# Splitting the output layers' loads in an attention-plus-feed-forward kernel: Wo stays inside the last chunk, the rest goes behind the last block moves

## The chip, the cores and the metric

The kernel runs on one core of a Trainium2 chip. The metric is the device time of one execution in microseconds. Before the change it is 712.91 us, the median of 3 runs (712.37 to 714.04).

## The reference, cut to what matters

One recurrent attention layer: 512 query rows (M) attend to 6250 input rows (x) with 8 heads of 64, and a feed-forward layer follows. All is fp32.

```python
q = (M @ Wq.T).reshape(e, h, dh).transpose(1, 0, 2)          # M 512x512
k, v = jnp.split(x @ Wkv.T + bkv, 2, axis=-1)                # x 6250x256
sim = jnp.einsum('hid,hjd->hij', q, k) * dh ** (-0.5)
sim = jnp.where(mask, sim, -1000000000.0)                    # mask 512x6250
attn = jax.nn.softmax(sim, axis=-1)
out = jnp.einsum('hij,hjd->hid', attn, v)
out = out.transpose(1, 0, 2).reshape(e, h * dh) @ Wo.T + bo  # Wo 512x512
m = layer_norm(out + M)
ffn = jax.nn.relu(m @ W1.T + b1) @ W2.T + b2                 # W1 2048x512, W2 512x2048
z = layer_norm(ffn + m)
```

## The kernel before, in words

The 6250 inputs are cut into 7 chunks of 896 (7 tiles of 128). In each chunk the 8 heads go in 4 pairs (0 to 3), and for each pair the 512 queries go in 4 tiles. Every engine walks through the same list of steps, written by hand in `ROUNDS` and turned into a list by `chunk_schedule`; it does those steps that have work for it and passes over the others. Engines meet at semaphores only. A step is written here as letter(pair, number), so X(3,2) is the transpose of pair 3, query tile 2. The steps around the change:

- S(p,t): TensorE (PE) makes the scores, VectorE (DVE) adds the mask and takes the minimum (line 669). E: ScalarE (ACT) takes the exponential (531). X(p,t): DVE transposes 32x32 blocks of the probabilities from `prob` to `st` (679). `st` has two halves, one for query tiles 0 and 1 and one for 2 and 3. X of an even tile waits until the DMAs that read this half for the pair before have landed (semaphores `landed`).
- M(p,g) and B(p,g): the blocks in half g are moved between partition groups, from `st` to `pt`, by 16 DMAs of 112 KB: 12 issued by SP's queue (M, line 350) and 4 by ACT's queue (B, line 567). In the text "move (p,g)" is all 16.
- W(p,kt): PE multiplies `pt` with the values (853). It starts only when both moves of its pair have landed. C copies the result out of the bank, F transposes it back, A adds it to the accumulator, N divides by the softmax sum, G, T and D turn and split the normalised output, and Y multiplies it with Wo (784).
- Z(p): GpSimd (POOL) updates the maxima and sums (423 to 434), ACT makes alpha (571).
- R and Q load the next x and mask. In the last chunk they are left out. There I stands instead (SP, lines 366 to 377) at the end of pair 2's last round: after a few waits SP issues Wo (1024 KB), M (`m_res`, 1024 KB), the first two tiles of W1 and of W2 (4 times 256 KB), and the biases bo and b2 spread over 128 partitions (2 times 256 KB). O stands at the end of pair 3's last round (POOL, 463 to 470): it splits Wo into a high and a low part (465, 467) and then adds bo to M (470).

After the list of the last chunk the output layers follow: ACT (577, 581) and DVE (709, 713) split the first feed-forward tiles, DVE adds `m_res` and gathers the statistics of the layer norm (701 to 705), PE turns the result (893), and 16 hidden tiles run through PE (904 and 912), whose weights SP loads two tiles ahead.

SP's queue is one list in program order. In the last chunk SP issues M(2,0), then I, then M(2,1), M(3,0) and M(3,1). The same stretch on POOL: Z(2), O, Z(3).

Of the kernel before, what the change touches and what calls it, by code (L numbers as in the profile page):

```python
# [12 lines left out]
P = 128  # L13
# [3 lines left out]
DM = 512  # L17
# [5 lines left out]
PAIRS = HEADS // 2  # L23
U = 2 * QT
KT = 7
CHUNK = KT * P
CHUNKS = -(-N // CHUNK)
# [44 lines left out]
def chunk_schedule(first, last):  # L72

    out = []
    for p in range(PAIRS):
        for t in range(QT):
            for word in ROUNDS[p][t].split():
                kind, i = word[0], int(word[1:] or 0)
                step = (kind, p, i)
                if kind == "S":  # L80
                    step = (kind, p, t)
                elif kind == "E":
                    step = (kind, p, (t, i))
                elif kind == "X":
                    step = (kind, p, t - 1) if t else (kind, p - 1, QT - 1)
                elif kind == "V":
                    step = (kind, 0, i)
                elif kind in "NP":
                    if kind == "P" and not first or kind == "N" and last:
                        continue  # L90
                    step = ("V", 1 if kind == "N" else 0, i)
                elif kind in "WC":
                    step = (kind, p - 2, i)
                elif kind in "FA":
                    step = (kind, p - 3, i)
                elif kind in "KHL":
                    step = (kind, p + 1, i)
                elif kind in "MB":
                    step = (kind, p - i, i)
                elif kind == "Z":  # L100
                    step = (kind, p - 1, i)
                if first and step[1] < 0 or last and (kind in "JRQ" or step[1] == PAIRS) or not last and kind in "IO":
                    continue
                out.append(step)
                if kind == "A" and last and step[1] >= 0:
                    out.append(("N", step[1], 0))
    if last:
        a, b = PAIRS - 2, PAIRS - 1
        out.extend([("F", 1, 0), ("A", 1, 0), ("N", 1, 0)])
        out.extend([("X", b, 3), ("M", b, 1), ("B", b, 1), ("Z", b, 0)])  # L110
        out.extend([("G", 0, 0), ("T", 0, 0), ("D", 0, 0)])
        out.extend([*(("W", a, kt) for kt in range(3)), ("G", 1, 0), ("T", 1, 0), ("D", 1, 0)])
        out.extend([*(("W", a, kt) for kt in range(3, KT)), ("C", a, 0), ("Y", 0, 0), ("F", a, 0), ("A", a, 0), ("N", a, 0)])
        out.extend([("Y", 0, 1), ("Y", 0, 2), ("Y", 0, 3), ("G", a, 0), ("T", a, 0), ("D", a, 0)])
        out.extend([*(("W", b, kt) for kt in range(KT)), ("C", b, 0), ("Y", 1, 0), ("F", b, 0), ("A", b, 0), ("N", b, 0)])
        out.extend([("Y", 1, 1), ("Y", 1, 2), ("Y", 1, 3), ("G", b, 0), ("T", b, 0), ("D", b, 0)])
        out.extend([("Y", 2, t) for t in range(QT)])
    return out


def build(nc, x, mask, mt, mn, wq, wk, wv, bk, bv, wo, bo, w1, b1, w2, b2, out):
    with ExitStack() as ctx:
# [198 lines left out]
        @block.sync  # L321
        def _(sp):
            sp.dma_start(wk_raw[:], wk).then_inc(wk_in, 16)
            for b in range(2):
                cols = slice(b * HALF, b * HALF + HALF)
                sp.dma_start((x_raw, x_late)[b][:], x[0, :, :, cols]).then_inc(x0_in[b], 16)
            for i in range(2):
                part = slice(i * MC // 2, (i + 1) * MC // 2)
                sp.dma_start(mt_raw[:, part], mt[:, part]).then_inc(mt_in[i], 16)
                sp.dma_start(wq_raw[:, part], wq[:, part]).then_inc(wq_in[i], 16)  # L330
            sp.dma_start(bk_sb[:], bk).then_inc(bk_in, 16)
            sp.dma_start(mask_raw[:], mask[0]).then_inc(mask_in, 16)
            sp.dma_start(wv_raw[:], wv).then_inc(wv_in, 16)
            sp.dma_start(bv_sb[:], bv).then_inc(bias_in, 16)
            sp.dma_start(b1_sb[:], b1).then_inc(bias_in, 16)

            def body(c, sched, parity):
                for kind, p, i in sched:
                    if kind == "M":
                        n, buf = pair_no(c, p), move_buf(p, i)  # L340
                        read = in_register(sp, KT * (n - 1)) if is_past(n, 2) else None
                        written = in_register(sp, QT * n + 2 * i + 2)
                        sp.wait_ge(wv_lo, 1)
                        if read is not None:
                            sp.wait_ge(pv_done, read)
                        sp.wait_ge(xposed, written)
                        for turn in (0, 1, 2):
                            for a in (0, 2, 1, 3):
                                b = (a + turn) % QUAD
                                sp.dma_start(pt[LANES * b:LANES * b + LANES, buf, a],  # L350
                                             st[LANES * a:LANES * a + LANES, i, b]).then_inc(landed[buf], 16)
                    if kind == "R":
                        taken = in_register(sp, x_taken(c) + i)
                        sp.wait_ge(zeroed, 2)
                        sp.wait_ge(xhi_ready, taken)
                        sp.wait_ge(xlo_ready, taken)
                        src = x[c + 1] if isinstance(c, int) else x[bass.ds(c + 1, 1)].rearrange("a p k n -> (a p) k n")
                        sp.dma_start(x_raw[:], src[:, :, i * HALF:i * HALF + HALF]).then_inc(x_in, 16)
                    if kind == "Q":
                        lowered = in_register(sp, (c + 1) * QT)  # L360
                        sp.wait_ge(zeroed, 2)
                        sp.wait_ge(lower_ready, lowered)
                        src = mask[c + 1] if isinstance(c, int) else mask[bass.ds(c + 1, 1)].rearrange("a p k n -> (a p) k n")
                        sp.dma_start(mask_raw[:], src).then_inc(mask_in, 16)
                    if kind == "I":
                        sp.wait_ge(filled[KEYS_RING], keys_use(pair_no(c, PAIRS - 1)) + 1)
                        sp.wait_ge(v_filled, KT * CHUNKS)
                        sp.wait_ge(lower_ready, CHUNKS * QT)
                        sp.wait_ge(klo_done, PAIRS * CHUNKS - 1)
                        sp.dma_start(wo_raw[:], wo).then_inc(wo_in, 16)  # L370
                        sp.dma_start(m_res[:], mn).then_inc(mres_in, 16)
                        for j in range(2):
                            sp.dma_start(w1_raw[:, j], w1[j]).then_inc(w1_in[j], 16)
                            sp.dma_start(w2_raw[:, j], w2[j]).then_inc(w2_in[j], 16)
                        sp.wait_ge(pv_done, KT * PAIRS * (CHUNKS - 1))
                        sp.dma_start(bo_sb[:], bo.to_broadcast([P, DM])).then_inc(bias_in, 16)
                        sp.dma_start(b2_sb[:], b2.to_broadcast([P, DM])).then_inc(bias_in, 16)

            chunks(sp, body)

            with sp.Fori(2, FT - 1, 2) as i:
                for j in range(2):
                    for taken in (w1hi, w1lo, w2hi, w2lo):
                        sp.wait_ge(taken, i - 1 + j)
                    sp.dma_start(w1_raw[:, j], w1[bass.ds(i + j, 1)].rearrange("a p k n -> (a p) k n")).then_inc(w1_in[j], 16)
                    sp.dma_start(w2_raw[:, j], w2[bass.ds(i + j, 1)].rearrange("a p n -> (a p) n")).then_inc(w2_in[j], 16)
            for t in range(QT):
                sp.wait_ge(z_ready, t + 1)
                sp.dma_start(out[t], norm[:, t]).then_inc(out_done, 16)
            sp.wait_ge(out_done, 16 * QT)  # L390

        @block.gpsimd
        def _(pool):
# [20 lines left out]
            def body(c, sched, parity):  # L414
# [4 lines left out]
                for kind, p, i in sched:  # L419
# [35 lines left out]
                    if kind == "S" and p == PAIRS - 1 and not final:  # L455
# [4 lines left out]
                            pool.wait_ge(mask_in, loaded)  # L460
                        pool.wait_ge(drained[j], read)
                        lower_tile(i)
                    if kind == "O":
                        pool.wait_ge(wo_in, 16)
                        nc.gpsimd.tensor_copy(wo2[0][:], wo_raw[:]).then_inc(wohi, 1)
                        pool.wait_ge(wohi, 1)
                        nc.gpsimd.tensor_tensor(wo2[1][:], wo_raw[:], wo2[0][:], ALU.subtract).then_inc(wolo, 1)
                        pool.wait_ge(mres_in, 16)
                        pool.wait_ge(bias_in, 16 * 4)
                        nc.gpsimd.tensor_tensor(m_res[:], m_res[:], bo_sb[:].unsqueeze(1).to_broadcast([P, QT, DM]), ALU.add).then_inc(mres_ready, 1)  # L470
# [505 lines left out]
```

## Time and profile before

| what | value |
|---|---|
| median of 3 runs | 712.91 us |
| the profiled execution: whole | 711.92 us |
| the profiled execution: span of the trace | 710.1 us |
| PE busy | 633.1 us, 89% |
| DVE busy | 552.7 us, 78% |
| ACT busy | 363.8 us, 51% |
| POOL busy | 245.5 us, 35% |
| mean granted TensorE clock | 0.977 |

The span runs from the first instruction to the last. Outside it lie 1.8 us. The chain of waits follows the work that ended last backwards, from each instruction to what released it. Times in the trace count from the start of the span.

### The profile page before, as it was taken

The numbers are of one execution on the slowest core, as the hardware profiler recorded it, in microseconds if no ns is written. First come the engines' busy times: TensorE is split into PE (matmuls) and PEld (weight loads), VectorE is DVE, ScalarE is ACT, GpSimd is POOL, SyncE is SP. The second block draws the span as 40 slices with busy tenths as digits, with TensorE's granted clock in tenths as the row PEclk, the third lists the DMA queues.
The fourth block names the chain that finished last, engine by engine and source line by source line (L and its number), as shares of the span: only waits on it lengthen the run. The fifth ranks groups of instructions, "written<-read, shape, count | busy, mean of one in ns | idle before, by whom it ended". The sixth has DMA issues, their size and how long they took to land.

```text
span 710.1 us, 11125 instructions
## 1 busy us (share of the span) xinstructions
PE 633.1 (89%) x3382; PEld 398.3 (56%) x3382; DVE 552.7 (78%) x688; ACT 363.8 (51%) x658; POOL 245.5 (35%) x305
## 2 busy tenths in 40 slices
PE   3967999999999999998999999999998287899995
PEld 3755556555556556554565566555564144688883
DVE  5378899989998999988998999899989345433333
ACT  5355566556665566654666555566564212433332
POOL 3212552246322632264225522463221601522223
PEclk9999999999999999999999999999999699899998
DMA  7038788988898889888797998888887960023311
GB/s 281 1 77 221 201 213 208 240 204 214 206 242 205 199 220 252 201 199 203 193 239 192 215 228 228 200 215 211 199 203 197 285 166 30 30 89 95 107 64 60
DMA packets 54938, 128.37 MB, mean 181 GB/s; under 512 B 15840, under 2 KB 19424, under 8 KB 54624
## 3 DMA queue, kind: packets, MB, share of 16 engines
q1 hardware_dynamic: 44128, 101.97, 56.1%
q10 hardware_dynamic: 10752, 25.70, 13.8%
q8 instruction: 27, 0.44, 0.3%
q14 instruction: 31, 0.25, 0.1%
HBM read 23.80 MB, written 1.05 MB: 35 GB/s over the span
## 4 chain that ended last, share of the span: by engine, by line
PE 42%; DVE 21%; SPq 14%; issue 9%; DMA 7%; ACT 3%; ACTq 2%; DVEq 1%; POOL 1%; POOLq 0%
SPq L350 14%; DVE st L679 11%; PE tail L853 9%; PE slot L825 8%; PE slot L904 6%; PE slot L912 6%; DMA pt<-st 6%; DVE prob L669 6%; PE slot L750 5%; PE tail L750 5%; ACT prob L531 2%; ACTq L567 2%; PE tail L860 1%; DMA wq_raw<-in_wq 1%; PE slot L784 1%
## 5 line engine op out<-in xcount | busy, mean ns | idle before, releaser
L531 ACT ACTIVATE prob<-prob,negmax 128x896 f32<-128x896 f32 x224 | 233.6, 1043 | 215.1 <-DVE negmax L669 192.6
L669 DVE CUSTOM_DVE_ANT_0 prob<-slot,lower,negmax_old 128x896 f32<-128x896 f32 x224 | 248.9, 1148 | 40.6 <-PE slot L825 28.3
L679 DVE STREAM_TRANSPOSE st<-prob 128x1792 f32<-128x1792 f32 x112 | 228.4, 2040 | 15.0 <-DMA pt<-st 14.6
L853 PE MATMUL tail<-pt,val 128*64 128x512 f32 x784 | 185.2, 606 | 17.2 <-DMA pt<-st 10.8
L853 PEld LDWEIGHTS tail<-pt,val 128*64 128x64 f32 x784 | 51.7, 138 | 113.4 <-issue 105.1
L825 PE MATMUL slot<-k_hi,q_hi 64*128 64x448 f32 x448 | 95.7, 416 | 19.5 <-DVE negmax L669 16.1
L825 PEld LDWEIGHTS slot<-k_hi,q_hi 64*128 64x128 f32 x448 | 44.0, 185 | 87.0 <-issue 77.7
L825 PE MATMUL slot<-k_hi,q_lo 64*128 64x448 f32 x448 | 85.4, 366 | 0.0
L825 PE MATMUL slot<-k_lo,q_hi 64*128 64x448 f32 x448 | 84.8, 364 | 0.0
L429 POOL TENSOR_TENSOR total<-total,alpha 128x8 f32<-128x8 f32 x28 | 5.8, 206 | 199.2 <-ACT alpha L571 199.2
L442 POOL TENSOR_TENSOR k_lo<-k_raw,k_hi 128x896 fp32r<-128x896 f32 x27 | 57.1, 2114 | 3.9 <-POOL k_hi L439 0.2
L404 POOL TENSOR_SCALAR lower<-mask_raw 128x896 bf16<-128x896 uint8 x28 | 27.2, 970 | 54.8 <-DVE negmax L669 42.9
L825 PEld LDWEIGHTS slot<-k_hi,q_lo 64*128 64x128 f32 x448 | 44.7, 186 | 2.4
L825 PEld LDWEIGHTS slot<-k_lo,q_hi 64*128 64x128 f32 x448 | 44.7, 187 | 1.0
L750 PE MATMUL tail<-wv_hi,x_hi 128*128 128x512 f32 x98 | 36.4, 453 | 8.6 <-ACT val L540 8.6
L476 POOL TENSOR_TENSOR hid_lo<-hid,hid_hi 128x512 fp32r<-128x512 f32 x16 | 21.3, 1332 | 65.4 <-DVE hid_hi L734 65.4
L531 ACT ACTIVATION_READ_ACCUMULATOR prob<-prob,negmax 128x1 f32 x224 | 41.8, 186 | 0.0
L750 PE MATMUL slot<-x_hi,wk_hi 128*128 128x448 f32 x112 | 33.3, 379 | 8.8 <-ACT x_hi L506 8.8
L734 DVE CAST hid_hi<-hid 128x512 fp32r<-128x512 f32 x16 | 6.8, 426 | 35.0 <-ACT hid L606 35.0
L750 PE MATMUL slot<-x_lo,wk_hi 128*128 128x448 f32 x112 | 32.6, 373 | 0.0
L750 PE MATMUL slot<-x_hi,wk_lo 128*128 128x448 f32 x112 | 32.5, 372 | 0.0
L750 PE MATMUL tail<-wv_lo,x_hi 128*128 128x512 f32 x98 | 31.1, 398 | 0.0
(112 smaller groups left out, 812.6 us busy)
## 6 DMA issues: line engine op xcount, KB each, us to landing
pt<-st SPq DMA_DIRECT2D x672, 112.0 KB, 3.1
pt<-st ACTq DMA_DIRECT2D x224, 112.0 KB, 3.4
w_raw<-in_w SPq DMA_DIRECT2D x32, 256.0 KB, 2.8
x_raw<-in_x SPq DMA_DIRECT2D x13, 448.0 KB, 4.0
mask_raw<-in_mask SPq DMA_DIRECT2D x7, 448.0 KB, 4.5
mt_raw<-in_mt SPq DMA_DIRECT2D x2, 512.0 KB, 7.6
wq_raw<-in_wq SPq DMA_DIRECT2D x2, 512.0 KB, 8.2
wo_raw<-in_wo SPq DMA_DIRECT2D x1, 1024.0 KB, 5.1
```

The source lines that it names most:

```text
L350: sp.dma_start(pt[LANES * b:LANES * b + LANES, buf, a], st[LANES * a:LANES * a + LANES, i, b]).then_inc(landed[buf], 16)
L404: nc.gpsimd.tensor_scalar(lower[:, t], mask_raw[:, t], -1.0, -BIG, ALU.add, ALU.mult).then_inc(lower_ready, 1)
L442: nc.gpsimd.tensor_tensor(kst[1][:, p % 2], k_raw[:], kst[0][:, p % 2], ALU.subtract).then_inc(klo_done, 1)
L476: nc.gpsimd.tensor_tensor(hid2[1][:, j], hid[:, j], hid2[0][:, j], ALU.subtract).then_inc(hidlo, 1)
L531: nc.scalar.activation(unit, unit, ACT.Exp, bias=negmax[:, p, u:u + 1], scale=-1.0, accum_out=psumrow[:, p, u:u + 1]).then_inc(exp_done, 1)
L669: nc.vector.tensor_tensor_reduce(out=prob[:, i % 2, h].rearrange("p (b n) -> p b n", b=2), in0=slot[:, j, :, :HALF], in1=lower[:, i].rearr ...
L679: nc.vector.transpose(st[:, g].rearrange("p b k (t i) -> p k b t i", t=2)[:, :, :, t2], prob[:, i % 2].rearrange("p h (k b i) -> p (h k) b ...
L750: last = nc.tensor.matmul(dst, stationary(a, k), moving(b, k), start=(n == 0), stop=(n == len(terms) - 1))
L825: last = nc.tensor.matmul(slot[:, j, b, :HALF], q2[qa][rows(h), p, P * i:P * i + P], key_half(p, b, kb)[rows(h)], start=(part == 0), stop= ...
L853: last = nc.tensor.matmul(outT[DH * h:DH * h + DH], val[:, val_at(i, parity ^ (p < 0)), head(p, h)], moving, start=(i == 0), stop=(i == KT ...
L904: last = nc.tensor.matmul(slot[:, 2, j], w12[a][:, j, k], mT2[b][:, k], start=(i == 0), stop=(i == len(terms) - 1))
L912: last = nc.tensor.matmul(slot[:, t // 2, t % 2], hid2[a][:, j, P * t:P * t + P], w22[b][:, j], start=first and i == 0, stop=last_one and ...
```

## The change: what it does

I and O get a second part. Part 0 keeps its place in the list: on SP it issues Wo alone, on POOL it splits Wo. Part 1 is put at the end of the block that closes pair 3's moves, behind X(3,3), M(3,1), B(3,1) and Z(3). On SP it issues M, then the two biases, then the first tiles of W1 and W2; on POOL it adds bo to M. The biases now stand ahead of the feed-forward tiles. No instruction is added or taken away.

```diff
         out.extend([("F", 1, 0), ("A", 1, 0), ("N", 1, 0)])
-        out.extend([("X", b, 3), ("M", b, 1), ("B", b, 1), ("Z", b, 0)])
+        out.extend([("X", b, 3), ("M", b, 1), ("B", b, 1), ("Z", b, 0), ("I", b, 1), ("O", b, 1)])
...
-                    if kind == "I":
+                    if kind == "I" and i == 0:
                         sp.wait_ge(filled[KEYS_RING], keys_use(pair_no(c, PAIRS - 1)) + 1)
                         sp.wait_ge(v_filled, KT * CHUNKS)
                         sp.wait_ge(lower_ready, CHUNKS * QT)
                         sp.wait_ge(klo_done, PAIRS * CHUNKS - 1)
                         sp.dma_start(wo_raw[:], wo).then_inc(wo_in, 16)
+                    if kind == "I" and i == 1:
                         sp.dma_start(m_res[:], mn).then_inc(mres_in, 16)
+                        sp.wait_ge(pv_done, KT * PAIRS * (CHUNKS - 1))
+                        sp.dma_start(bo_sb[:], bo.to_broadcast([P, DM])).then_inc(bias_in, 16)
+                        sp.dma_start(b2_sb[:], b2.to_broadcast([P, DM])).then_inc(bias_in, 16)
                         for j in range(2):
                             sp.dma_start(w1_raw[:, j], w1[j]).then_inc(w1_in[j], 16)
                             sp.dma_start(w2_raw[:, j], w2[j]).then_inc(w2_in[j], 16)
-                        sp.wait_ge(pv_done, KT * PAIRS * (CHUNKS - 1))
-                        sp.dma_start(bo_sb[:], bo.to_broadcast([P, DM])).then_inc(bias_in, 16)
-                        sp.dma_start(b2_sb[:], b2.to_broadcast([P, DM])).then_inc(bias_in, 16)
...
-                    if kind == "O":
+                    if kind == "O" and i == 0:
                         pool.wait_ge(wo_in, 16)
...
+                    if kind == "O" and i == 1:
                         pool.wait_ge(mres_in, 16)
                         pool.wait_ge(bias_in, 16 * 4)
```

SP's queue in the last chunk before (the 72 moves are the last of the chunk before and M(0,0) to M(2,0), the 36 are M(2,1), M(3,0) and M(3,1); `w_raw` stands for the W1 and W2 tiles in turn):

```order
L350 DMA pt<-st 32x896 x72
L370 DMA wo_raw<-in_wo 128x2048
L371 DMA m_res<-in_mn 128x2048
L373 DMA w_raw<-in_w 128x512
L374 DMA w_raw<-in_w 128x512
L373 DMA w_raw<-in_w 128x512
L374 DMA w_raw<-in_w 128x512
L376 DMA bo_sb<-in_bo 128x512
L377 DMA b_sb<-in_b 128x512
L350 DMA pt<-st 32x896 x36
L381 UNCONDITIONAL_BRANCH
```

The same stretch of SP's queue in the changed kernel:

```order
L350 DMA pt<-st 32x896 x72
L370 DMA wo_raw<-in_wo 128x2048
L350 DMA pt<-st 32x896 x36
L372 DMA m_res<-in_mn 128x2048
L374 DMA bo_sb<-in_bo 128x512
L375 DMA b_sb<-in_b 128x512
L377 DMA w_raw<-in_w 128x512
L378 DMA w_raw<-in_w 128x512
L377 DMA w_raw<-in_w 128x512
L378 DMA w_raw<-in_w 128x512
L382 UNCONDITIONAL_BRANCH
```

Seven DMAs (2560 KB) have moved from ahead of the last 36 moves to behind them; only Wo stays ahead.

POOL before, from the split of Wo to the first instruction of the layer norm:

```order
L465 CAST wo_hi<-wo_raw 128x2048 [waits wo_in]
L467 TENSOR_TENSOR wo_lo<-wo_raw,wo_hi 128x2048 [waits wohi_s]
L470 TENSOR_TENSOR m_res<-m_res,bo_sb 128x2048 [waits bias_in,mres_in]
L423 TENSOR_TENSOR drop<-negmax,negmax_old 128x8 [waits exp_done]
L427 COPY negmax_old<-negmax 128x8 [waits drop_ready,zeroed]
L429 TENSOR_TENSOR total<-total,alpha 128x8 [waits alpha_ready]
L431 TENSOR_TENSOR total<-total,psumrow 128x8 [waits total_scaled]
L434 TENSOR_TENSOR acc<-acc,alpha 128x512 [waits acc_added]
L480 TENSOR_SCALAR var_eps<-meanvar 128x1 [waits var_ready]
```

The same stretch of POOL in the changed kernel:

```order
L466 CAST wo_hi<-wo_raw 128x2048 [waits wo_in]
L468 TENSOR_TENSOR wo_lo<-wo_raw,wo_hi 128x2048 [waits wohi_s]
L424 TENSOR_TENSOR drop<-negmax,negmax_old 128x8 [waits exp_done]
L428 COPY negmax_old<-negmax 128x8 [waits drop_ready,zeroed]
L430 TENSOR_TENSOR total<-total,alpha 128x8 [waits alpha_ready]
L432 TENSOR_TENSOR total<-total,psumrow 128x8 [waits total_scaled]
L435 TENSOR_TENSOR acc<-acc,alpha 128x512 [waits acc_added]
L472 TENSOR_TENSOR m_res<-m_res,bo_sb 128x2048 [waits bias_in,mres_in]
L482 TENSOR_SCALAR var_eps<-meanvar 128x1 [waits var_ready]
```

The addition of bo to M has moved from ahead of Z(3) to behind it, and is now the last thing on POOL before the layer norm.

## Rows read from the trace of the kernel before

**Rows 1.** The page's chain that ended last, by engine and by line.

```profile
PE 42%; DVE 21%; SPq 14%; issue 9%; DMA 7%; ACT 3%; ACTq 2%; DVEq 1%; POOL 1%; POOLq 0%
```

**Rows 2.** The chain in order of time, 545 to 712: start us, us, what.

```profile
556.66 0.59 SPq L350
...
557.30 11.10 DMA pt<-st
...
579.12 1.63 PE slot L784 x6
...
585.74 6.16 PE tail L853 x28
```

**Rows 3.** Timeline of DVE, 552 to 600: start, us, instruction [idle before <-releaser].

```profile
552.61 2.04 DVE L679 STREAM_TRANSPOSE st<-prob 128x1792 f32<-128x1792 f32 x1
...
556.92 0.08 DVE L669 DVE_READ_ACCUMULATOR2_ANT negmax<- 128x1 f32 x1
568.42 2.04 DVE L679 STREAM_TRANSPOSE st<-prob 128x1792 f32<-128x1792 f32 x1 [11.41 <-DMA pt<-st]
...
571.86 2.04 DVE L679 STREAM_TRANSPOSE st<-prob 128x1792 f32<-128x1792 f32 x1
...
599.03 0.68 DVE L701 TENSOR_TENSOR norm<-slot,m_res 128x512 f32<-128x512 f32 x1
```

**Rows 4.** Timeline of SP's queue, 524 to 590: what it issues, and when.

```profile
545.57 0.46 SPq L370 DMA_DIRECT2D wo_raw<-in_wo  x1
546.08 0.44 SPq L371 DMA_DIRECT2D m_res<-in_mn  x1
...
549.67 0.60 SPq L377 DMA_DIRECT2D b_sb<-in_b  x1
550.39 31.13 SPq L350 DMA_DIRECT2D pt<-st  x36
```

**Rows 5.** The same queue in narrower windows: M(3,0), and the first of M(3,1).

```profile
558.00 7.84 SPq L350 DMA_DIRECT2D pt<-st  x12
...
573.98 1.14 SPq L350 DMA_DIRECT2D pt<-st  x2
```

**Rows 6.** Windows: engines' busy us, then granted clock, DMA share, GB/s.

```profile
545.60:550.70 5.10, 3.69 (x16) 2.22 (x18) 4.86 (x9) 2.31 (x5) 1.44 (x3) 0.68 0.94 295
550.70:561.10 10.40, 4.78 (x30) 2.31 (x26) 6.17 (x9) 4.88 (x9) 6.46 (x2) 0.83 1.03 307
561.10:568.40 7.30, 0.00 (x0) 0.00 (x0) 0.00 (x0) 0.00 (x0) 4.84 (x3) 0.50 1.05 252
...
573.90:582.70 8.80, 6.55 (x32) 3.72 (x29) 2.71 (x5) 1.84 (x4) 1.42 (x3) 1.00 0.87 209
```

**Rows 7.** DMA view, 561.1 to 568.4: queues (q1 SP's, q10 ACT's), packets, MB, share.

```profile
q1 hardware_dynamic: 576, 1.38, 78.6%
q10 hardware_dynamic: 192, 0.46, 26.8%
```

**Rows 8.** DMA view, 545.6 to 550.7: one queue moved, and issues with median us to landing.

```profile
q1 hardware_dynamic: 264, 1.51, 93.9%
...
wo_raw<-in_wo SPq DMA_DIRECT2D x1, 1024.0 KB, 5.1
...
pt<-st SPq DMA_DIRECT2D x1, 112.0 KB, 10.8
```

**Rows 9.** DMA view, 575 to 583: SP's moves of M(3,1) and their landing.

```profile
pt<-st SPq DMA_DIRECT2D x11, 112.0 KB, 3.3
```

**Rows 10.** Timeline of ACT, 540 to 612: start, us, instruction [idle before <-releaser].

```profile
557.04 1.04 ACT L531 ACTIVATE prob<-prob,negmax 128x896 f32<-128x896 f32 x1
...
596.43 1.12 ACT L577 CAST w_hi<-w_raw 128x512 fp32r<-128x512 f32 x2
```

**Rows 11.** Timeline of POOL, 500 to 612: start, us, instruction [idle before <-releaser].

```profile
552.73 4.57 POOL L467 TENSOR_TENSOR wo_lo<-wo_raw,wo_hi 128x2048 fp32r<-128x2048 f32 x1
561.21 4.49 POOL L470 TENSOR_TENSOR m_res<-m_res,bo_sb 128x2048 f32<-128x2048 f32 x1 [3.91 <-DMA b_sb<-in_b]
```

## The prediction

> **What bounds the kernel now.** I read the page's chain first. TensorE has 42% of it and DVE 21%, but 7% is a DMA [rows 1]. For a kernel that is otherwise dense this is the entry to explain. The chain in order of time puts one piece of 11.10 us of it at 557.30 [rows 2], behind an issue of SP that ends at 557.25. So the thing waited for is the last of M(2,1)'s twelve DMAs, issued then and landed at 568.4. The timeline of DVE names the waiter. It finished its last score minimum at 557.00 and then stood still for 11.41 us until X(3,2) began at 568.42 [rows 3]. X(3,2) writes the half of `st` that move (2,1) reads, so it needs that move landed. Its data was there: the exponentials of tile 2 come before those of tile 3, whose last one starts at 557.04 [rows 10]. Nothing else held X(3,2).
>
> What comes behind X(3,2) hangs on it in one line. X(3,3) follows at 571.86 and ends at 573.90 [rows 3]; ACT then issues B(3,1) and splits the first two outputs; Y begins at 579.12; W(3) at 585.74 [rows 2]; the layer norm begins at 599.03 [rows 3]. From there on the output layers have no input from the attention part. So if X(3,2) comes earlier by d, the whole rest comes earlier by d, until something else ends last.
>
> Why did the move land so late? SP's queue shows the order [rows 4]. Behind M(2,0) came Wo at 545.57, M at 546.08, five more loads, and b2 until 550.27; only at 550.39 did M(2,1) begin. Its X(2,3) was long done. The windows show the rest [rows 6]. The DMA engines were full (share 0.94, 1.03, 1.05) from 545.6 to 568.4. b2 landed just before 561.1, as GpSimd's wait for it ended at 561.21 [rows 11]. In the 7.30 us from 561.1 to 568.4 SP's queue moved 1.38 MB and ACT's 0.46 MB [rows 7]. Twelve moves of 112 KB are 1.376 MB, so that window is M(2,1) complete, with B(3,0) beside it, and all of it came behind the loads. A move issued at 550.4 took 10.8 us to land [rows 8], where one with no load ahead takes 3.3 us [rows 9].
>
> The Trainium skill ("DMA: Bandwidth & Descriptors", Queues, rings and completion order) says that on each DMA engine descriptors are consumed in the order of a queue's ring and that several queues take turns. The trace agrees: M(2,1)'s 1.38 MB pass after the loads' bytes, with ACT's 0.46 MB among them.
>
> **The change part by part.** No engine instruction is added or removed, and the lists of PE, DVE and ACT stay as they are.
>
> 1. Seven loads (2560 KB, 2.62 MB) leave SP's queue ahead of M(2,1). SP's issue time for them was 546.08 to 550.27, 4.2 us. M(2,1) now begins at 546.1. Twelve issues take 7.84 us [rows 5], so the last is issued at 553.9. With no backlog it lands 3.3 us later [rows 9], at 557.2. That is one bound.
>
> 2. There is still a backlog, Wo. By 550.7 SP's queue had moved 1.51 MB, the rest of M(2,0) and Wo [rows 8]; ACT's queue has no entry in that window. Wo landed 5.1 us after 545.57, at 550.7. I take that as unchanged. What is left of move (2,1) at 550.7 is then all of it, 16 times 112 KB or 1.84 MB. The same amount took 7.30 us in 561.1 to 568.4, at 252 GB/s [rows 6]. Landing: 550.7 + 7.3 = 558.0. This is my value, because it is the nearest row: the same bytes over the same two queues. At the pace of the slowest row, 209 GB/s, it would be 550.7 + 8.8 = 559.5. The other end is 557.0, when DVE itself comes free. X(3,2) at 558.0 instead of 568.42 gives 10.4 us. The ends are 8.9 us and 11.4 us.
>
> 3. M(3,0) follows. Its X(3,1) ends at 554.65 [rows 3] and SP is free at 553.9, so it is issued from 554.7 to 562.5. Its bytes come behind those of (2,1): 558.0 + 7.3 = 565.3. X(3,3) ends at 573.90 - 10.4 = 563.5. M(3,1) is issued from 563.5, 0.6 us for each, to 571.1. In the trace it took from 573.98 to 582.7 until the last byte, 8.7 us [rows 5, 6]; behind the backlog it is 565.3 + 7.3 = 572.6. W(3) needs it at 585.74 - 10.4 = 575.3. So the moves keep 2.7 us of cover, and cost nothing. If this cover were gone, each us late would be one us of PE.
>
> 4. The loads now stand behind M(3,1), on a queue that has nothing else to do until the feed-forward loop. They are issued from 571.1 to 575.3 and cannot delay a move any more. Their bytes start at about 572.6. M and the biases are 1.57 MB: 5.1 us at the 307 GB/s at which loads ran [rows 6], landing at 577.7; at 209 GB/s 580.1. POOL adds bo in 4.49 us [rows 11], done at 582.2 (584.6). DVE wants the result at 599.03 - 10.4 = 588.6. Cover: 6.4 us (4.0). All seven loads, 2.62 MB: 8.5 us, at 581.1; at 209 GB/s 585.1. ACT wants the first W1 tile at 596.43 - 10.4 = 586.0 [rows 10]. Cover: 4.9 us (0.9). So these loads cost nothing either, but this is where the thinnest cover lies if DMAs are slow.
>
> 5. POOL: m_res goes behind Z(3). Z(3) had waited behind it (it started at 565.7) and goes ahead now; what it needs from ACT comes later in both kernels. Nothing on POOL stands behind m_res until the layer norm. Value 0. From both sides: 4.49 us could at worst lie bare if the biases landed at the moment DVE asks; a gain is excluded, as nothing on the path waited for POOL here. The split of Wo ends at 557.3 [rows 11], 11 us ahead of Y even after the shift.
>
> 6. TensorE's clock: granted 0.50 in 561.1 to 568.4, while PE had no work, which is the 1.2 GHz level, and 1.00 in the window that starts at 573.90 [rows 6]. PE work right after the stall ran at the low level, but the path in that stretch runs over DVE and ACT, so I count 0. With a wait of 1 us instead of 11, it can at most be a few tenths better.
>
> A second rule of the Trainium skill speaks against the change. In the same page, Rules for kernel authors, it advises to issue a DMA early and wait on it late. By it the old place was the right one, and the new one risks a bare load. By the rows the loads were needed at 586 at the earliest and lay ready from 561 on, so the rule prices only the cover in step 4; followed by itself it would give no gain, the 711.9 of before.
>
> **Sum.** 711.92 us (span 710.1 and 1.8 outside it) - 10.4 = 701.5 us. The profiled execution lies 1.0 us below the median of the runs, 712.91; from that the same term gives 702.5. I put the forecast halfway, 702.0 us. Its own range is 711.92 - 11.4 = 700.5 to 712.91 - 8.9 = 704.0.
>
> **Rivals.**
>
> a) Wo alone is enough to stall. Wo is 1.05 MB, and the small moves behind it may run worse than I think, or W(3)'s moves may use up their 2.7 us. For it speaks that the four batches now run without a pause from 550.7 on. Against it: 252 GB/s is measured on these very moves. If they ran at 209 GB/s, three batches from 550.7 would end at 550.7 + 3 x 8.8 = 577.1. That is X(3,2) at 559.5 (8.9 us) and W(3) at 577.1 where 576.8 is asked, so a gain of 8.6. With Wo landing 2 us later as well, the gain is 6.6: 711.92 - 6.6 = 705.3 us.
>
> b) The change doesn't do what it says: M(2,1) was late for another reason than the loads. Then X(3,2) still stands at about 568 and the time is 711.9. For it: the wait is named as pt<-st, not as a load. Against it: the bytes by queue, and 10.8 against 3.3 us to landing.
>
> c) Slower. The deferred loads become the wait. The place is ACT's split of the first W1 tile (line 577), which blocks ACT, DVE's split behind it and the layer norm. The price is its lateness past 586.0. It turns the sign when the tiles land after 596.4, 25.3 us after the first is issued. That would be 2.62 MB at about 104 GB/s; at 90 GB/s it is 3.8 us later than that, 715.7 us. For it: the loads are now at the last possible place, beside nothing else that could hide them. Against it: no busy window here is below 209 GB/s.
>
> d) A part of c: loads land 3 to 4 us past 586.0. Then 701.5 + 3.5 = 705.0.
>
> **How the numbers follow.** Forecast 76%, a 10%, b 3%, c 2%, d 9%. A measurement of this kernel can tell about 0.2%, 1.4 us. The forecast, a and d are all faster by more than that: 0.95. b is no change: 0.03. c is slower: 0.02. The range should reach from the lower end of the forecast's own to a and d: 700.4 to 705.4. What it leaves out is b, c and the tails.
>
> **What would show it.** In the changed kernel's timeline SP issues Wo and then at once M(2,1) at about 546.1. DVE's wait before X(3,2) shrinks from 11.41 to about 1 us, with X(3,2) at 558.0. The chain of waits has hardly any DMA entry near 558. Y begins near 568.7, W(3) near 575.3, the layer norm near 588.6. m_res lands near 578, and POOL adds bo between 578 and 583 while DVE does not need it. ACT does not wait for a load before line 577's work. The feed-forward part keeps its length from the first norm to the end, 111.1 us. The forecast is wrong if DVE's wait stays above 3 us, if PE waits for pt<-st before W(3), or if ACT, DVE or POOL wait for a load after 580.

## The result, and the profile after

The changed kernel takes 702.38 us, the median of 4 runs (699.52 to 703.79), where the kernel before took 712.64 us in 4 runs (710.70 to 714.04). The two medians are 10.3 us apart. The recorded ratio, which counts from here on, is 0.9872 with a 95% interval of 0.9846 to 0.9899: faster by 9.1 us, 7 to 11. The forecast was 702.0. The profiled execution took 701.80 us, with a span of 700.0 us.

The page's chain by engine, against [rows 1]:

```profile
PE 57%; DVE 18%; issue 8%; SPq 7%; DMA 4%; ACT 3%; ACTq 2%; DVEq 1%; POOL 1%; POOLq 0%
```

TensorE has more of the chain and the DMAs and SP's queue less. Little of that is the change, though. The first experiment below has the whole stall back, and its page reads

```profile
PE 54%; DVE 18%; SPq 9%; issue 8%; DMA 5%; ACT 3%; ACTq 2%; DVEq 1%; POOL 1%; POOLq 0%
```

So the shares of the whole chain are no measure of one stall; its pieces are. The timeline of SP's queue after, against [rows 4]:

```profile
543.21 0.46 SPq L370 DMA_DIRECT2D wo_raw<-in_wo  x1
543.77 27.23 SPq L350 DMA_DIRECT2D pt<-st  x36
571.04 0.59 SPq L372 DMA_DIRECT2D m_res<-in_mn  x1
571.67 0.44 SPq L374 DMA_DIRECT2D bo_sb<-in_bo  x1
572.16 0.43 SPq L375 DMA_DIRECT2D b_sb<-in_b  x1
572.63 0.73 SPq L377 DMA_DIRECT2D w_raw<-in_w  x1
```

M(2,1) now begins 0.56 us after Wo, where it began 4.82 us after it. The timeline of DVE, against [rows 3]:

```profile
551.06 2.04 DVE L681 STREAM_TRANSPOSE st<-prob 128x1792 f32<-128x1792 f32 x1
...
557.38 2.05 DVE L681 STREAM_TRANSPOSE st<-prob 128x1792 f32<-128x1792 f32 x1 [1.91 <-DMA pt<-st]
...
588.25 0.68 DVE L703 TENSOR_TENSOR norm<-slot,m_res 128x512 f32<-128x512 f32 x1
```

The wait before X(3,2) fell from 11.41 to 1.91 us. The chain in order of time, against [rows 2]:

```profile
551.78 5.58 DMA pt<-st
...
562.96 0.52 ACTq L569
...
566.76 1.42 DVE ao_lo L697 x2
...
568.32 1.63 PE slot L786 x6
...
574.93 6.16 PE tail L855 x28
```

The DMA piece is down from 11.10 to 5.58 us, and most of that lay beside DVE's work. From X(3,2) on the chain has the same pieces as before: Y begins 10.94 us behind X(3,2) (10.70 before), W(3) 17.55 us behind it (17.32 before).

POOL after, against [rows 11]:

```profile
549.88 1.90 POOL L466 CAST wo_hi<-wo_raw 128x2048 fp32r<-128x2048 f32 x1 [1.69 <-DMA wo_raw<-in_wo]
...
578.82 4.56 POOL L472 TENSOR_TENSOR m_res<-m_res,bo_sb 128x2048 f32<-128x2048 f32 x1 [11.08 <-DMA b_sb<-in_b]
```

The addition ended at 583.4, and DVE asked for it at 588.25. The spans differ by 10.1 us. That splits at the rows shown: 1.55 us lie ahead of X(3,1) (552.61 against 551.06), 9.50 us are DVE's shorter wait, and 0.95 us were given back behind it: 0.26 us from X(3,2) to the layer norm, 0.68 us from there to the end, and 0.01 of rounding. (In the last of these stretches the granted clock stood at 0.50 for 10.2 us, 592.8 to 603.0, where it had for 6.8 us, 605.5 to 612.3, before. That this is the 0.68 us is likely and not shown.) Whether the first 1.55 us belong to the change is asked below.

### The profile page after: what moved, and what is told of

The parts are those of the page before. It is cut to its first block, busy times and chain, and to the rows that moved or that the text cites. A ratio compares the mean times of both kernels' runs of the same rounds, so it can differ in the third digit from the quotient of the medians.

```text
span 700.0 us, 11125 instructions
## 1 busy us (share of the span) xinstructions
PE 633.1 (90%) x3382; PEld 397.7 (57%) x3382; DVE 552.6 (79%) x688; ACT 364.3 (52%) x658; POOL 246.0 (35%) x305
## 3 DMA queue, kind: packets, MB, share of 16 engines
HBM read 23.80 MB, written 1.05 MB: 35 GB/s over the span
## 4 chain that ended last, share of the span: by engine, by line
PE 57%; DVE 18%; issue 8%; SPq 7%; DMA 4%; ACT 3%; ACTq 2%; DVEq 1%; POOL 1%; POOLq 0%
PE tail L855 14%; PE slot L827 12%; DVE st L681 8%; PE tail L752 8%; PE slot L752 7%; PE slot L906 6%; SPq L350 6%; PE slot L914 6%; DVE prob L671 5%; DMA pt<-st 2%; PE tail L862 2%; ACT prob L533 2%; ACTq L569 2%; DMA wq_raw<-in_wq 1%; PE slot L786 1%
## 5 line engine op out<-in xcount | busy, mean ns | idle before, releaser
L752 PE MATMUL tail<-wv_hi,x_lo 128*128 128x512 f32 x98 | 31.1, 399 | 0.0
```

The lines of the kernel that those rows point to most:

```text
L752: last = nc.tensor.matmul(dst, stationary(a, k), moving(b, k), start=(n == 0), stop=(n == len(terms) - 1))
```

## The experiments

The theory: SP's queue passes bytes in its own order, so each load ahead of M(2,1) delays its landing by its bytes, and what is behind the last move costs nothing until its cover is used up. The rivals: the order on POOL made the gain; SP's issue time counts and not the bytes; small moves are not held by large loads. In the fences `-` is the changed kernel and `+` the experiment; `...` marks lines left out. All edits are to the changed kernel.

**The POOL part alone.**

```diff
-     'S E0 E1 W5 W6 C X B0 J1 I'),
+     'S E0 E1 W5 W6 C X B0 J1 I I1'),
...
-        out.extend([("X", b, 3), ("M", b, 1), ("B", b, 1), ("Z", b, 0), ("I", b, 1), ("O", b, 1)])
+        out.extend([("X", b, 3), ("M", b, 1), ("B", b, 1), ("Z", b, 0), ("O", b, 1)])
```

> The changed kernel with its seven loads put back directly behind Wo, ahead of M(2,1); the addition of bo to M stays behind Z(3). So this is the POOL part of the change alone. Theory (backlog: the moves stand behind the loads' bytes on SP's queue): the stall is back, DVE waits some 11.4 us before X(3,2) and the time is that of before, 712.6 us within 1.5. Rival (the addition ahead of Z(3) held POOL, and with it alpha and the chain): the gain stays, 702.4 us, with a DVE wait near 1.9 us.

711.66 us (10 runs), ratio to before 1.0005 (0.9981 to 1.0029). DVE's timeline has the stall back:

```profile
566.48 2.05 DVE L681 STREAM_TRANSPOSE st<-prob 128x1792 f32<-128x1792 f32 x1 [10.83 <-DMA pt<-st]
```

So POOL's order brings nothing by itself, and the stall hangs on what stands in SP's queue. Whether SP's part is enough alone is the next question. Issue time can't be the whole cause: M(2,1) began 4.98 us after Wo (549.11 against 544.13), 4.4 us later than in the changed kernel, and DVE waited 8.9 us longer.

The trace of the kernel before also tells a queue's order from a mere sharing of the DMA engines. A move of ACT's own queue, issued at 548.88, landed at 557.23; a move of SP's queue, issued at 550.39, landed only at 561.21, just after the last load (561.07). So ACT's moves were slowed by the loads but went past them, and SP's moves stood behind all of them. No run puts the loads on another queue, so what they would cost there stays open.

**The SP part alone.**

```diff
-     'S E0 E1 N0 X B0 O'),
+     'S E0 E1 N0 X B0 O O1'),
...
-        out.extend([("X", b, 3), ("M", b, 1), ("B", b, 1), ("Z", b, 0), ("I", b, 1), ("O", b, 1)])
+        out.extend([("X", b, 3), ("M", b, 1), ("B", b, 1), ("Z", b, 0), ("I", b, 1)])
```

> The changed kernel with the addition of bo to M back in its old place on POOL, ahead of Z(3); the seven loads stay behind the last moves. So this is the SP part alone. Theory: DVE's wait before X(3,2) stays near 2 us, but POOL now waits for the biases (landed at 578.8 in the changed kernel), adds for 4.6 us until 583.4, and only then starts Z(3), on which ACT's alpha and the split of the first two outputs hang. Alpha goes from 566 to 584, Y from 568.3 to 586: 18 us lost, 720.4 us, slower than before. Rival (nothing on the path hangs on POOL here): 702.4 us.

723.31 us (4 runs), ratio 1.0175 (1.0119 to 1.0231): slower than before. The waits of its last chunk:

```profile
ACT alpha L573 <- POOL drop L424: 26.8, 1, 26.8
POOL m_res L472 <- DMA b_sb<-in_b: 22.0, 1, 22.0
```

DVE's wait before X(3,2) was 1.69 us, so the first half of the gain was there. But POOL stood before the addition for 22.0 us, with Z(3) queued behind it, and alpha on ACT stood for 26.8. Y began at 587.31 after 19.75 us of idle TensorE. The move of O is not idle housekeeping: it is what makes the late loads free. The time is 2.9 us above the expected one, and against the kernel before, which took 710.76 us in this group, it is 12.5 us slower where 7.8 were expected. The spans of the two profiles (721.4 and 700.0) differ by 21.4 us: Y began 19.0 us later (587.31 against 568.32), and from the start of Y to W(3) it took 9.28 us, where the changed kernel took 6.54; the clock is taken up below.

**The loads between M(2,1) and M(3,0).**

```diff
-    ('S E0 E1 W0 W1 W2 W3 X M1',
+    ('S E0 E1 W0 W1 W2 W3 X M1 I1',
...
-        out.extend([("X", b, 3), ("M", b, 1), ("B", b, 1), ("Z", b, 0), ("I", b, 1), ("O", b, 1)])
+        out.extend([("X", b, 3), ("M", b, 1), ("B", b, 1), ("Z", b, 0), ("O", b, 1)])
```

> The changed kernel with the seven loads between M(2,1) and M(3,0) instead of behind M(3,1). Theory (bytes pass in the order of the queue): X(3,2) is as in the changed kernel, near 557.4 with a wait of about 2 us. Then 2.62 MB at 307 GB/s take 8.5 us, moves (3,0) and (3,1) 7.3 us each: the last lands at 557.4 + 8.5 + 14.6 = 580.5, where W(3) asked at 574.9. PE waits 5.6 us for pt<-st ahead of W(3), time 708.0 us. Rival (small moves and large loads share the DMA engines, so a move is not held by loads ahead of it): no wait at W(3), 702.4 us.

709.30 us (10 runs), ratio 0.9978 (0.9958 to 0.9999): most of the gain is gone, and more than expected (708.0). PE's timeline, at W(3):

```profile
580.07 7.92 PE L855 MATMUL tail<-pt,val 128*64 128x512 f32 x28 [4.01 <-DMA pt<-st]
```

X(3,2) is free (it starts at 558.95), and the wait has gone to W(3), at 580.07 where 580.5 was worked out. The bytes in the order of the queue give the right instant. The price of the wait is higher than its 4.01 us. The windows of this kernel show why; their last columns are granted clock, DMA share and GB/s:

```profile
576.00:580.00 4.00, 0.06 (x1) 0.00 (x0) 0.75 (x1) 0.69 (x1) 0.00 (x0) 1.00 0.49 149
580.00:582.00 2.00, 1.93 (x8) 0.87 (x10) 0.00 (x0) 0.00 (x0) 0.00 (x0) 0.80 0.00 0
582.00:584.00 2.00, 2.00 (x6) 0.60 (x4) 0.00 (x0) 0.00 (x0) 0.00 (x0) 0.50 0.00 0
```

After PE had stood still, the granted clock fell to 0.50 (1.2 GHz) inside W(3), and its 28 matmuls took 7.92 us instead of 6.23. That is 1.7 us on top, 5.7 in all, of the 6.3 us by which the spans of the two profiles differ (706.3 and 700.0).

**M alone ahead of the moves.**

```diff
+                        sp.dma_start(m_res[:], mn).then_inc(mres_in, 16)
                     if kind == "I" and i == 1:
-                        sp.dma_start(m_res[:], mn).then_inc(mres_in, 16)
```

> The changed kernel with M (m_res, 1.05 MB) alone put back behind Wo, the other six loads stay behind the last moves. A dose between the two kernels. Theory (bytes): 1.05 MB at 307 GB/s, 3.4 us more of backlog, DVE's wait before X(3,2) goes from 1.9 to 5.3 us, time 705.8 us. Rival (it is the time that SP takes to issue, 0.5 us for this one load, that delays the move): wait 2.4 us, 702.9 us.

704.43 us (9 runs), ratio 0.9913 (0.9892 to 0.9935). DVE's timeline:

```profile
558.75 2.05 DVE L681 STREAM_TRANSPOSE st<-prob 128x1792 f32<-128x1792 f32 x1 [4.29 <-DMA pt<-st]
```

The wait is 4.29 us, between the two theories' 5.3 and 2.4, and nearer to the bytes. With 0, 1.05 and 2.62 MB of deferred loads put back, DVE waits 1.91, 4.29 and 10.83 us: 3.4 us for each MB over the whole way, which is 294 GB/s. That is a rate from two single executions, and the middle point is not on the line: 2.3 us for the first MB, 4.2 for each of the rest. The next experiment shows that the wait without M scatters up to 3.48 us, so this one wait alone would not decide. The ratio helps: 0.9913 is about 3 us slower than the changed kernel (0.9872 and 0.9866), where the bytes asked for 3.4 us and issue time for 0.5.

**The changed kernel again.**

> The changed kernel once more, as the reference of this group. Its profile put X(3,1) 1.55 us earlier than in the kernel before, ahead of anything that the change touches. Theory (that part is scatter of one execution): here X(3,1) starts anywhere within 1.5 us of 552, DVE's wait before X(3,2) is again near 1.9 us, and the gain against before is the 9.5 us of the shortened wait less a few tenths, a ratio near 0.988. Rival (the change also speeds the stretch ahead of it): X(3,1) starts at 551.1 again and the ratio is 0.985.

701.54 us (6 runs), ratio 0.9866 (0.9843 to 0.9889), 9.5 us. X(3,1) started at 550.18 here. In the ten profiles of this study beside the two first ones it starts between 550.06 and 552.55, at 551.25 for the POOL part alone, which is as slow as before. So the 1.55 us ahead of X(3,1) are scatter of one execution. The ratio, 0.9866, lies between the two expected ones (0.988 and 0.985) and decides nothing. The wait before X(3,2) was 0.96 us. It scatters too: 1.91, 0.96, 1.69, 2.80, 1.12 and 3.48 us in six executions with only Wo ahead of the move. A second thing came out of this profile, its chain at Y:

```profile
566.48 2.80 PE slot L786 x6
569.28 0.85 PE tail L862 x4
570.13 4.13 PE slot L786 x18
```

Six matmuls took 2.80 us instead of the 1.63 of the first profile. The windows of the two executions, this one first:

```profile
566.40:568.00 1.60, 1.52 (x4) 1.26 (x5) 0.00 (x0) 0.00 (x0) 0.00 (x0) 0.56 0.89 222
568.00:570.00 2.00, 2.00 (x9) 1.60 (x8) 0.00 (x0) 0.00 (x0) 0.00 (x0) 0.50 0.79 174
```

```profile
568.30:570.00 1.70, 1.68 (x8) 1.39 (x9) 0.00 (x0) 0.00 (x0) 0.00 (x0) 1.00 1.00 238
```

The same kernel ran the start of Y at 0.50 in one execution and at 1.00 in the other. That costs 1.6 us (566.48 to W(3) at 574.63 is 8.15 us, against 6.54), and is one part of the spread of 4 to 5 us between runs, beside X(3,1)'s start and the wait before X(3,2), which scatter by 2.5 us each.

**Wo behind M(2,1) too.**

```diff
-     'S E0 E1 W5 W6 C X B0 J1 I'),
-    ('S E0 E1 W0 W1 W2 W3 X M1',
+     'S E0 E1 W5 W6 C X B0 J1'),
+    ('S E0 E1 W0 W1 W2 W3 X M1 I',
```

> The changed kernel with Wo too behind M(2,1) instead of ahead of it. Theory: the 1.9 us that DVE still waits before X(3,2) are Wo's bytes, so the wait is below 0.3 us. But Wo lands about 4 us after M(2,1), and its split (6.4 us on POOL, ahead of Z(3)) ends near 566, so alpha on ACT waits for POOL until then; the time is within 1 us of the changed kernel. Rival (the rest of the wait is the SP's issue time of twelve moves and their own bytes): the wait stays above 1.5 us.

703.08 us (4 runs), ratio 0.9872 (0.9844 to 0.9900), the same as the changed kernel. DVE had no wait before X(3,2). POOL's and ACT's rows in this kernel's waits are

```profile
POOL wo_hi L466 <- DMA wo_raw<-in_wo: 10.3, 1, 10.3
...
ACT alpha L573 <- POOL drop L424: 8.8, 1, 8.8
```

So the remaining wait is Wo's bytes, as the theory has it: 0 us here lies below all six of the waits above. Taking it away gains nothing, because the split of Wo then ends at 566.2 and holds Z(3). In this execution the first matmuls of Y ran at the low clock too, as in the one above (8.15 us from Y to W(3)).

**The loads later still.**

```diff
                     if kind == "I" and i == 1:
+                        sp.wait_ge(outT_copied, PAIRS * CHUNKS)
```

> The changed kernel with the seven loads held back until ACT has copied out the product of pair 3 (a wait of SP on that copy, at about 581.7 instead of 571.0). This measures the cover of the loads. Theory: b2 lands 5.9 to 7.6 us after the first issue, at 587.6 to 589.3, POOL's addition of 4.56 us ends at 592.2 to 593.9, and DVE asks at 588.25: 4.0 to 5.6 us lost, 706.4 to 708.0 us, with DVE's layer norm waiting for POOL. Rival (the W1 tile on ACT is the first to miss, as the prediction had it): the loss is the same or less, but ACT's line 579 shows the wait for w_raw, and DVE waits for ACT and not for POOL's m_res.

709.02 us (10 runs), ratio 0.9973 (0.9960 to 0.9985): 7.5 us above the changed kernel of the same group, more than either theory said. POOL, ACT and DVE in this kernel:

```profile
589.31 4.51 POOL L473 TENSOR_TENSOR m_res<-m_res,bo_sb 128x2048 f32<-128x2048 f32 x1 [21.70 <-DMA b_sb<-in_b]
590.03 0.62 ACT L580 CAST w_hi<-w_raw 128x512 fp32r<-128x512 f32 x1 [4.43 <-DMA w_raw<-in_w]
590.68 4.29 DVE L712 TENSOR_TENSOR w_lo<-w_raw,w_hi 128x512 fp32r<-128x512 f32 x2 [4.30 <-ACT w_hi L580]
...
594.89 0.68 DVE L716 TENSOR_TENSOR w_lo<-w_raw,w_hi 128x512 fp32r<-128x512 f32 x1
595.49 0.68 DVE L704 TENSOR_TENSOR norm<-slot,m_res 128x512 f32<-128x512 f32 x1
```

The first to miss is ACT's split of W1, by 4.43 us, as the rival had it. Then comes something that neither had: DVE's two splits took 4.29 us instead of 1.28. They began while POOL's addition ran (589.31 to 593.82) and did not get through before its end. The layer norm began 43.76 us behind X(3,1), against 37.19: 6.6 us. Of these, 4.9 us last until the addition ends (593.82), the wait that the theory named and within its 4.0 to 5.6, and 1.7 us are the two splits and what follows them behind it.

**The addition beside DVE's splits.**

```diff
                     if kind == "O" and i == 1:
+                        pool.wait_ge(norm_ready, PAIRS)
```

> The changed kernel with POOL's addition of bo to M held back until N(3) is done (about 584.2), so that it runs beside DVE's split of the first feed-forward tiles (lines 711 and 715, near 586.4, all operands in SBUF). Two experiments before this one showed DVE instructions with all operands in SBUF stretched until a POOL instruction on SBUF ended: 1.68 us instead of 0.69, and two of line 712 in 4.29 us instead of 1.28. Theory (such a DVE instruction doesn't run beside the POOL one): the addition runs from 584.2 to 588.7, the three splits (2.0 us) take place behind it, the layer norm begins near 590.7 instead of 588.25, 2.4 us slower than the changed kernel. Rival (they run side by side and the stretch was something else): the splits take 0.68 us each, the layer norm waits only for the end of the addition, 588.8, 0.6 us slower.

705.07 us (4 runs), ratio 0.9915 (0.9893 to 0.9938).

```profile
587.72 3.56 DVE L712 TENSOR_TENSOR w_lo<-w_raw,w_hi 128x512 fp32r<-128x512 f32 x2
591.21 0.68 DVE L716 TENSOR_TENSOR w_lo<-w_raw,w_hi 128x512 fp32r<-128x512 f32 x1
```

```profile
585.56 4.57 POOL L473 TENSOR_TENSOR m_res<-m_res,bo_sb 128x2048 f32<-128x2048 f32 x1 [16.56 <-DVE acc L695]
```

No load was late here, and the two splits again end 1.15 us, about the length of two, behind the end of the addition at 590.13. The layer norm begins 41.05 us behind X(3,1). Of the 3.86 us more, 1.57 are a longer wait before X(3,2) in this execution, and 2.3 are the collision; 2.4 was expected. The rival, 0.6 us, falls.

**Gathers earlier, at the new bound.**

```diff
-        out.extend([("F", 1, 0), ("A", 1, 0), ("N", 1, 0)])
+        at = out.index(("X", b, 2))
+        out[at:at] = [("F", 1, 0), ("A", 1, 0), ("N", 1, 0)]
+        out.extend([("G", 0, 0), ("T", 0, 0), ("G", 1, 0), ("T", 1, 0)])
         out.extend([("X", b, 3), ("M", b, 1), ("B", b, 1), ("Z", b, 0), ("I", b, 1), ("O", b, 1)])
-        out.extend([("G", 0, 0), ("T", 0, 0), ("D", 0, 0)])
-        out.extend([*(("W", a, kt) for kt in range(3)), ("G", 1, 0), ("T", 1, 0), ("D", 1, 0)])
-        out.extend([*(("W", a, kt) for kt in range(3, KT)), ("C", a, 0), ("Y", 0, 0), ("F", a, 0), ("A", a, 0), ("N", a, 0)])
+        out.extend([("D", 0, 0), ("D", 1, 0)])
+        out.extend([*(("W", a, kt) for kt in range(KT)), ("C", a, 0), ("Y", 0, 0), ("F", a, 0), ("A", a, 0), ("N", a, 0)])
```

> The changed kernel with another order at its new bound: F(1), A(1), N(1) go ahead of X(3,2), into the time that DVE waits there; G(0), T(0), G(1), T(1) go ahead of X(3,3) and B(3,1), so that ACT splits the first two outputs before it issues the four DMAs of B(3,1); D(0) and D(1) follow X(3,3). Theory (after the change the chain runs over DVE and ACT's queue from X(3,2) to Y): X(3,3) starts 1.5 us earlier, Y is ready 5 us earlier and waits only for PE, W(3) starts near 572.5 instead of 574.9, where move (3,1) lands: 2 to 2.4 us faster, 700.2 us. Rival (the backlog of moves is the bound already): PE waits for pt<-st before W(3) and the gain is below 1 us, 702 us.

700.36 us (5 runs), ratio 0.9853 (0.9835 to 0.9870). It is the lowest median of the study, 1.2 us below the changed kernel of the same group, but the intervals overlap, so better than the changed kernel is likely and not shown. W(3) began at 572.35 without a wait for a DMA, as expected. DVE's rows tell what was lost:

```profile
555.91 1.68 DVE L695 TENSOR_TENSOR acc<-acc,inv 128x512 f32<-128x512 f32 x1
...
581.00 1.68 DVE L695 TENSOR_TENSOR acc<-acc,inv 128x512 f32<-128x512 f32 x1
```

Two multiplications of N, N(1) and N(3), collide with POOL, one with the split of Wo (until 557.04), one with the addition (until 582.13). Each takes 1.0 us more than 0.69.

**b2 behind the feed-forward tiles, on top of it.** The load of b2 goes behind the W tiles with its own semaphore, on which POOL waits only where it uses b2; its addition of bo waits for M and bo.

```diff
-                        sp.dma_start(b2_sb[:], b2.to_broadcast([P, DM])).then_inc(bias_in, 16)
...
+                        sp.dma_start(b2_sb[:], b2.to_broadcast([P, DM])).then_inc(b2_in, 16)
...
-                        pool.wait_ge(bias_in, 16 * 4)
+                        pool.wait_ge(bias_in, 16 * 3)
```

> The kernel with the early gathers (e8) and b2 moved behind the first feed-forward tiles with a semaphore of its own, so that POOL's addition waits only for M and bo. In e8 this addition ran from 577.54 to 582.13 and DVE's N(3) at 581.00 took 1.68 us instead of 0.69. Theory (collision of the two): the addition starts 0.6 us earlier, N(3) takes 1.1 us, and the time is 0.5 us below e8: 699.8 us, about 11 us below before, ratio 0.9845. Rival (N(3) was late for another reason): no change in N(3), 700.4 us.

701.29 us (4 runs), ratio 0.9868 (0.9847 to 0.9890): no gain over the kernel above that can be told. The second collision is gone (N(3) at 582.91 took 0.69 us), but the first grew: N(1) took 2.11 us. The addition started 26.5 us behind X(3,1), 0.3 us earlier than in the kernel above (26.9). N(3) came 1.3 us later (31.6 us behind X(3,1), against 30.3), and it is this that let it miss the addition, which ended 31.1 us behind X(3,1). So the run says nothing for or against the 0.5 us.

## Why the prediction was right, point by point

- **The bound.** Right, and shown from both sides. The loads back in their place alone bring the whole stall back (10.83 us, ratio 1.0005), a part of them costs a part of the gain, and the same loads one move later move the wait to W(3) at the instant that their bytes give.
- **Step 1, issue time.** M(2,1) began 0.56 us after Wo, 0.5 expected. The pace of issue was not a bound. (The bound of 557.2 was read 0.6 us too late: the view counts the 3.3 us from the start of an issue, and the step put them behind its end. The sum does not use it.)
- **Step 2, the landing.** The wait was put at about 1 us (558.0 against 557.0) and was 1.91, 0.96 in the second execution. Its two terms are both slightly off. The bytes of the move held: from Wo's landing to X(3,2) it took 7.5 us (549.8 to 557.38), 7.3 expected. But Wo itself, taken as unchanged at 5.1 us, landed after 6.6 us. The DMA view of 545.6 to 550.7 now has ACT's moves in it, where it had none [rows 8]:

```profile
q1 hardware_dynamic: 311, 1.30, 85.1%
q10 hardware_dynamic: 76, 0.19, 15.6%
```

  Part of that lies behind Wo's landing, as Wo came earlier here. Over Wo's own time, 543.2 to 549.85, SP's queue moved 1.66 MB and ACT's 0.09, at 263 GB/s; before, 545.57 to 550.7, it was 1.51 MB, all SP's, at 294 GB/s. So Wo had 0.24 MB of moves beside it and a lower rate. It is no scatter: Wo took 5.0 to 5.1 us in the three kernels with a further load right behind it (before, the first experiment and the fourth), and 5.9 to 7.1 us in the nine profiles with moves behind it.

  So the wait fell by 9.5 us in the first pair of profiles, where 10.4 were put down. The term whose size was off is Wo's landing, 5.1 us put down and 6.6 measured.
- **Step 3, cover of the moves.** W(3) began at 574.86 (575.3 expected) with no DMA wait. The last move was issued at 570.4 and landed 2.2 us later, at 572.6, the instant that the step gives, so the cover was 2.2 us, 2.7 expected. What a late move would cost was too low: "one us of PE" for each us. The run with the loads in the middle waited 4.01 us and paid 5.7, since the clock fell.
- **Step 4, cover of the loads.** b2 landed at 578.7 (577.7), the addition ended at 583.4 (582.2), DVE asked at 588.25 (588.6): cover 4.9 us, 6.4 expected. All seven were there at 581.4 (581.1), and ACT asked at 585.64 (586.0). Loads issued 10.6 us later cost 7.5 us.
- **Step 5, POOL.** Value 0 was right for the changed kernel. But the step named only the case in which the biases land too late; the order of the two parts had a far larger price, 21.4 us between the profiles if O had not moved along. And a collision of the addition with DVE was not thought of. The changed kernel misses it narrowly: the addition ends at 583.38, and the multiplication of N(3), the next DVE instruction that reads two tensors in SBUF, starts at 583.51.
- **Step 6, the clock.** It was counted as 0 on the path. It is not always 0: 1.6 us at Y in one of two profiles of the same kernel.
- **The sum.** 9.5 us of wait less 0.95 us behind it is 8.6 us for the change proper in the first pair of profiles; the recorded ratios say 9.1 and 9.5. The forecast's 10.4 us was 1 to 2 us too much. That the median came out within 0.4 us of the forecast is partly luck: the first pair of profiles has 1.55 us that do not belong to the change, and the halfway point between profile and median alone was worth half a us.
- **The rivals.** a (more of the stall stays) is there in small, as 1 to 3.5 us of wait instead of 1. b falls by the first experiment. c and d did not happen; the delay experiment shows their mechanism at its place, ACT's split of W1 (a wait of 4.43 us), but there the addition's end and the collision set the layer norm. The rule of the Trainium skill ("DMA: Bandwidth & Descriptors", Rules for kernel authors) to issue a DMA early and wait late would have kept the old order. Here that order was worth nothing, for the seven loads had landed by 561.1 and nothing on the path needed them before 596.4, 35 us later; and it cost 9 us, as the moves stood behind them.

## What to carry to other kernels

In this kernel a load that was issued early was free only where nothing urgent stood behind it on the same queue. For another kernel, add up the bytes between an urgent transfer and its turn, divide by the measured rate, and compare with when its waiter is ready. When a load is deferred, the instruction that waits for it must be deferred on its own engine too, past everything that others need from that engine. And the cover of a deferred piece is measured to the first of its waiters and with the engines that share a path with it, not only to the largest one.

## What the runs showed of the hardware that was not expected

- A DVE instruction that reads two tensors in SBUF did not run beside a POOL instruction that does. Where the DVE one began second, it was recorded long and ended 0.55 us behind POOL's: the multiplication of N in four kernels, with early gathers and without (1.44 to 2.11 us instead of 0.69, five times), and the splits of W1 in two. The kernel before has it too, in its feed-forward part: twelve splits of weight tiles took 0.86 to 1.78 us instead of 0.69, beside POOL's split of the hidden tiles. There, at 614.96, a DVE split that began together with POOL's took its 0.69, and POOL's took 1.84 us instead of 1.30. DVE instructions that read one tensor in SBUF were not held: in the kernel with early gathers an addition of A, whose other operand is in PSUM, ran at 555.01 in 0.68 us, and a reciprocal at 555.61 in 0.20, both inside POOL's split of Wo (552.51 to 557.04). The trace agrees with the Trainium skill ("SBUF — State Buffer", Who interferes with whom), which says that a DVE instruction with two SBUF inputs contends with a GpSimd instruction that reads SBUF, that the port pair which they share is an exclusive lock, and that a DVE instruction with at most one SBUF input, outside the modes that use both ports, does not contend.
- TensorE's granted clock after idle times of about 2 us was 0.50 in some executions and 1.00 in others: idle for 1.60, 1.72 and 2.25 us before Y it stayed high, for 2.01 and 2.16 us it was low. Length alone does not decide it here.
- ACT's four moves, on a queue of their own, do not escape the backlog either: before the change they took 7.9 us to land when issued near 558, into the backlog, and 3.5 us near 575, with no load ahead. They did get past SP's loads, as told with the first experiment.
